# Feed-forward of a transformer layer: the full square of each relu block made by ScalarE instead of GpSimd

## The chip, the cores and the metric

One core of a Trainium2 chip runs the whole layer in one launch. The metric is the device time of that launch in microseconds; the time of the kernel before is the median of three runs, 1094.78 us. Its five engines work side by side and meet at semaphores: TensorE (PE, matmuls and weight loads), VectorE (DVE), ScalarE (ACT), GpSimd (POOL) and SyncE (SP, which issues the DMAs).

## What is computed

A pre-norm layer on x of 4 x 2048 rows of 256: attention in a window of 128 keys with one global key (16 heads of 16), then a feed-forward with ternary weights, a low-rank term and a squared relu.

```python
x = x + attention(layernorm(x), Wq, Wk, Wv, Wo)
# feed-forward on xn = layernorm(x): 256 -> 1024 -> 256
h = bitlinear(xn, w_fc) + gate * (xn @ v.T @ fast_b.T @ u.T)
r = maximum(h, 0.0)
x = x + bitlinear(r * r, w_proj)
```

## The kernel before

The program has three stages: projections (to about 124 us), attention (to about 722 us) and the feed-forward (`stage_feed`, to the end). The change is in the feed-forward alone. There the 8192 rows are cut into 16 groups of 512 (`G`), and the 1024 hidden columns into 8 blocks of 128 (`MH`, index j). Every tile of a block is 128 partitions x 512 elements.

Products run in a fast matmul format, so a value that needs full precision is split in two: a high part (rounded, fp32r) and a low part (value minus high part), with a matmul for each. For the square this takes four steps per block, and the texts below use these short names:

- **T(j)**, `pe_ternary` and `pe_low` (L1827, L1828, L1832): five matmuls that make block j of h in one of two PSUM banks, `h_bank[j % 2]`. T(j) waits until relu j-2 has read that bank (`s_r`).
- **r(j)**, L1879, ScalarE: relu from PSUM into `f_relu`. **hi(j)**, L1882, ScalarE: its Square, rounded, into `f_square_hi`; it waits for r(j).
- **sq(j)**, L1890, GpSimd: r times r in full fp32, into `f_square`; it waits for r(j).
- **lo(j)**, L1936, VectorE: `f_square` minus `f_square_hi` into `f_square_lo`; it waits for hi(j) and sq(j). **O(j)**, `pe_output` (L1846, L1848): eight matmuls with both parts; it waits for lo(j).

The tiles of r, hi, sq and lo are rings of four blocks. Each engine takes its work in the order in which it is written; nothing else orders it. One step of the loop (`body`) handles the feed-forward of group q.g, the layernorm of the group after it (`qx`) and the output projection of attention of the group after that (`qa`):

- TensorE: low-rank product (L1818, L1819), T(0), T(1), eight transposes (L1784), T(2), T(3), O(0), T(4), O(1), T(5), O(2), T(6), O(3), T(7), O(4), eight transposes (L1796), O(5), 24 matmuls of the output projection (L257 to L259), O(6), O(7).
- ScalarE: the copy of the low-rank product f_z (L1872), r and hi of blocks 0 and 1, a square root for the layernorm (L161, "the root"), r(2), hi(2), two copies f_o_t_hi (L1861), r and hi of blocks 3 to 7, two copies f_xt_hi (L1867).
- VectorE: the output rows of the group before, the low part of f_z, layernorm statistics (L146, L154, L157), lo(0), lo(1), a chain of five small operations on 4 elements (L167 to L175), lo(2), two low parts (L1902), lo(3), scaling (L247), lo(4), scaling, lo(5) to lo(7), two low parts (L1923), two sums (L1910).
- GpSimd: sq(j) and nothing else, for j = 0 to 7.

Steps 0 to 13 have both `qa` and `qx`; step 14 has no `qa` (no transposes L1784, no copies L1861), step 15 has neither.

Of the kernel before, what the change touches and what calls it, by code (L numbers as in the profile page):

```python
# [24 lines left out]
ACT = mybir.ActivationFunctionType  # L25
ALU = mybir.AluOpType
# [10 lines left out]
MH = HID // P  # L37
# [4 lines left out]
G = N // GT  # L42
# [49 lines left out]
def wait(eng, sem, value):  # L92

    if value > 0:
        eng.wait_ge(sem, value)
# [1595 lines left out]
class Feed:  # L1691
# [182 lines left out]
    def act_squares(self, act, q, j):  # L1874
        sh = self.sh
        act.wait_ge(self.s_h, q.g * MH + j + 1)
        wait(act, self.s_sq, q.g * MH + j + 1 - 4)
        wait(act, self.s_y, q.g * MH + j + 1 - 4)
        act.activation(sh.r[:, j % 4, :], self.h_bank[j % 2][:], ACT.Relu, scale=self.w.mag[:, j:j + 1]  # L1879
                       ).then_inc(self.s_r, 1)  # L1880
        act.wait_ge(self.s_r, q.g * MH + j + 1)
        act.activation(sh.r2_hi[:, j % 4, :], sh.r[:, j % 4, :], ACT.Square).then_inc(self.s_r2hi, 1)  # L1882

    def pool_squares(self, pool, q, j):
        sh = self.sh
        pool.wait_ge(self.s_r, q.g * MH + j + 1)
        wait(pool, self.s_r2lo, q.g * MH + j + 1 - 4)
        pool.tensor_tensor(sh.r2[:, j % 4, :], sh.r[:, j % 4, :], sh.r[:, j % 4, :], ALU.mult).then_inc(self.s_sq, 1)  # L1890

# [69 lines left out]
def stage_feed(block, feed):  # L1963

    sh, norm = feed.sh, feed.norm
    LX, LF, LB = 1, 2, 3

    def steps(body):
        for i in range(LF, G + LB):
            body(lambda lag, i=i: Group(i - lag) if 0 <= i - lag < G else None)

    @block.sync
    def _(sp):
        feed.load_o(sp, Group(1))
        feed.load_x(sp, Group(1))
        feed.load_o(sp, Group(2))
        feed.load_x(sp, Group(2))  # L1980

        def body(at):
            if q := at(LB):
                if q.g == G - 1:
                    feed.store_last(sp, q)
                else:
                    feed.store(sp, q)
            if q := at(-1):
                feed.load_o(sp, q)
                feed.load_x(sp, q)  # L1990
                if q.g == 4:
                    feed.store_attention(sp)

        steps(body)
        for i in range(4):

            sp.wait_ge(feed.s_out[i], DMA * (G // 4 + (i == (G - 1) % 4)))

    @block.gpsimd
    def _(pool):  # L2000
        for g in range(G):
            for j in range(MH):
                feed.pool_squares(pool, Group(g), j)

    @block.tensor
    def _(pe):
        def body(at):
            qa, qx, qf = at(0), at(LX), at(LF)
            if qf:
                feed.pe_low_rank(pe, qf)  # L2010
                feed.pe_ternary(pe, qf, 0)
                feed.pe_ternary(pe, qf, 1)
                feed.pe_low(pe, qf, 0)
                feed.pe_low(pe, qf, 1)
            if qa:
                feed.pe_turn_o(pe, qa, qf)
            if qf:
                for j in range(2, MH):
                    feed.pe_ternary(pe, qf, j)
                    feed.pe_low(pe, qf, j)  # L2020
                    if j >= 3:
                        feed.pe_output(pe, qf, j - 3)
            if qx:
                feed.pe_turn_norm(pe, qx)
            if qf:
                feed.pe_output(pe, qf, MH - 3)
            if qa:
                feed.pe_attention(pe, qa)
            if qf:
                feed.pe_output(pe, qf, MH - 2)  # L2030
            if qf and qf.g == G - 1:

                for c in range(2):
                    feed.pe_output(pe, qf, MH - 1, (c,))
            elif qf:
                feed.pe_output(pe, qf, MH - 1)

        steps(body)

    @block.scalar  # L2040
    def _(act):
        def body(at):
            qa, qx, qf = at(0), at(LX), at(LF)
            if qf:
                feed.act_z_high(act, qf)
            for j in range(MH):
                if qf:
                    feed.act_squares(act, qf, j)
                if j == 1 and qx:
                    norm.root(act, qx)  # L2050
                if j == 2 and qa:
                    feed.act_o_high(act, qa)
            if qx:
                feed.act_norm_high(act, qx)

        steps(body)

    @block.vector
    def _(dve):
        def body(at):  # L2060
            qa, qx, qf, qb = at(0), at(LX), at(LF), at(LB)
            if qb and qb.g == G - 1:
                feed.dve_last(dve, qb)
            elif qb:
                feed.dve_scaled(dve, qb)
            if qf:
                feed.dve_z_low(dve, qf)
            if qb and qb.g < G - 1:
                feed.dve_final(dve, qb)
            if qx:  # L2070
                feed.dve_front(dve, qx)
            if qf and qf.g == 0:
                sh.dve_denominators(dve, Unit(UNITS - 1))
            for j in range(MH):
                if qf:
                    feed.dve_square_low(dve, qf, j)
                if j == 1 and qx:
                    norm.rstd(dve, qx)
                if j == 2 and qa:
                    feed.dve_o_low(dve, qa)  # L2080
                if j in (3, 4) and qx:
                    feed.dve_scale(dve, qx, range((j - 3) * 2, (j - 3) * 2 + 2))
            if qx:
                feed.dve_norm_low(dve, qx)
            if qa:
                feed.dve_x1(dve, qa)

        steps(body)


def layer(nc, x, wq, wk, wv, wo, fast_b, w_fc, w_proj, u, v, gate, out):
    q_dram = nc.dram_tensor("q_parts", [G, PARTS, HD, UPG // KT, NQ, KT, GT], BF16, kind="Internal").ap()
    k_dram = nc.dram_tensor("k_parts", [G, PARTS, HD, UPG // KT, NQ, KT, KGT], BF16, kind="Internal").ap()
    va_dram = nc.dram_tensor("v_ones", [N, VROW], F32, kind="Internal").ap()
    o_dram = nc.dram_tensor("attention", [N, D], F32, kind="Internal").ap()
    with ExitStack() as outer:
        row = outer.enter_context(nc.sbuf_tensor("row", [B, H, HD], F32))
        band = outer.enter_context(nc.sbuf_tensor("band", [P, -(-WINDOW // 16) * 16], BF16))
        with ExitStack() as place:
            weights = Weights(nc, outer, wo, fast_b, w_fc, w_proj, u, v, gate)  # L2100
            sh = Shared(nc, outer, place, row, band, Weights.WORDS)
        stage_project(nc, x, (wq, wk, wv), q_dram, k_dram, va_dram, o_dram, weights, sh)
        sh.keep(nc, outer)
        feed = Feed(nc, outer, x, o_dram, sh, weights, out)
        block = outer.enter_context(nc.Block())
        stage_attend(nc, outer, block, q_dram, k_dram, va_dram, o_dram, sh, weights, feed)
        stage_feed(block, feed)
# [22 lines left out]
```

## Time and profile before

| | |
|---|---|
| three runs | 1094.78, 1091.4, 1096.73 us |
| the profiled execution | 1093.67 us, of which the span of the core is 1091.9 us |
| busy over the span | PE 96%, DVE 84%, ACT 71%, POOL 64% |
| one group of the feed-forward | 23.07 us: PE 22.76, DVE 19.42, ACT 12.98, POOL 9.09 us busy |

The engines overlap, so their busy times do not add up to the span. What counts is which engine the others wait for at a given place, and what it waits for.

### The profile page before, as it was taken

The numbers are of one execution on the slowest core, as the hardware profiler recorded it, in microseconds if no ns is written. First come the engines' busy times: TensorE is split into PE (matmuls) and PEld (weight loads), VectorE is DVE, ScalarE is ACT, GpSimd is POOL, SyncE is SP. The second block draws the span as 40 slices with busy tenths as digits, with TensorE's granted clock in tenths as the row PEclk, the third lists the DMA queues.
The fourth block names the chain that finished last, engine by engine and source line by source line (L and its number), as shares of the span: only waits on it lengthen the run. The fifth ranks groups of instructions, "written<-read, shape, count | busy, mean of one in ns | idle before, by whom it ended". The sixth has DMA issues, their size and how long they took to land.

```text
span 1091.9 us, 40107 instructions
## 1 busy us (share of the span) xinstructions
PE 1043.6 (96%) x16091; PEld 788.7 (72%) x16091; DVE 918.9 (84%) x3205; ACT 772.6 (71%) x1325; POOL 700.3 (64%) x948
## 2 busy tenths in 40 slices
PE   9999998899999999999999999779999999999997
PEld 8888885456665666556665666458888888888887
DVE  7889965799899998999989999368878888888885
ACT  7989984488788878888878888645545655456654
POOL 3665559388889888998888888734334444334443
PEclk9999998699999999999999999989999999999999
DMA  6999989656767667666767752412122311113101
GB/s 206 282 306 275 288 231 231 131 118 122 146 145 152 139 131 156 149 137 132 154 126 156 138 119 69 138 39 78 59 59 75 99 59 59 59 59 97 40 21 39
DMA packets 185290, 142.34 MB, mean 130 GB/s; under 512 B 59896, under 2 KB 184848, under 8 KB 185104
## 3 DMA queue, kind: packets, MB, share of 16 engines
q1 hardware_dynamic: 185104, 139.77, 53.0%
q8 instruction: 127, 2.08, 0.9%
q14 instruction: 59, 0.48, 0.2%
HBM read 87.98 MB, written 50.95 MB: 127 GB/s over the span
## 4 chain that ended last, share of the span: by engine, by line
PE 62%; DVE 12%; issue 4%; ACT 2%; DMA 1%; POOL 1%; SPq 0%; POOLq 0%; DVEq 0%
PE e_psum L1534 14%; PE e_psum L1556 12%; PE e_psum L1509 10%; PE e_psum L1846 6%; PE e_psum L1848 6%; DVE a_masked L1665 5%; PE e_psum L1828 3%; PE e_psum L1827 3%; DVE n_stats L146 2%; DVE f_x L1960 2%; PE e_psum L1832 1%; PE e_psum L259 1%; PE e_psum L258 1%; ACT a_weights L1622 1%; PE e_psum L1796 1%
## 5 line engine op out<-in xcount | busy, mean ns | idle before, releaser
L1622 ACT ACTIVATE a_weights<-e_psum 128x1024 f32<-128x1024 f32 (+1 forms) x512 | 391.8, 809 | 86.0 <-PE e_psum L1534 85.7
L1665 DVE CUSTOM_DVE_ANT_0 a_masked<-e_psum,band 128x290 f32<-128x290 f32 (+8 forms) x1024 | 399.8, 445 | 44.2 <-PE e_psum L1509 37.9
L1439 POOL TENSOR_SCALAR_AFFINE_SELECT a_weights<-a_weights 128x1024 f32<-128x1024 f32 x256 | 273.4, 1092 | 52.3 <-ACT a_weights L1622 51.3
L1890 POOL TENSOR_TENSOR f_square<-f_relu 128x512 f32<-128x512 f32 x128 | 146.3, 1144 | 209.4 <-ACT f_relu L1879 186.7
L1509 PE MATMUL e_psum<-e_k,e_q 96*32 96x290 bf16 (+2 forms) x4096 | 233.3, 289 | 14.9 <-DVE a_max L1665 7.3
L1534 PE MATMUL e_psum<-e_q,e_k 128*32 128x256 bf16 (+2 forms) x5632 | 239.4, 280 | 7.3 <-ACT a_weights L1622 4.3
L1556 PE MATMUL e_psum<-a_weights,a_v 128*17 128x384 f32 (+2 forms) x2816 | 219.9, 392 | 7.7 <-DVE e_turned L1291 6.4
L1534 PEld LDWEIGHTS e_psum<-e_q,e_k 128*32 128x32 bf16 x5632 | 128.1, 96 | 101.8 <-ACT a_weights L1622 44.7
L1509 PEld LDWEIGHTS e_psum<-e_k,e_q 96*32 96x32 bf16 x4096 | 113.1, 97 | 86.0 <-DVE a_max L1665 51.6
L1846 PE MATMUL e_psum<-w_w_t,f_square_hi 128*128 128x256 f32 x512 | 129.3, 287 | 5.7 <-DVE f_square_lo L1936 5.7
L1848 PE MATMUL e_psum<-w_w_t,f_square_lo 128*128 128x256 f32 x512 | 126.7, 282 | 0.0
L1879 ACT ACTIVATE f_relu<-e_psum,w_mag 128x512 f32<-128x512 f32 x128 | 87.3, 682 | 54.2 <-PE e_psum L1832 54.2
L1936 DVE TENSOR_TENSOR f_square_lo<-f_square,f_square_hi 128x512 fp32r<-128x512 f32 x128 | 98.4, 788 | 24.2 <-POOL f_square L1890 24.2
L1846 PEld LDWEIGHTS e_psum<-w_w_t,f_square_hi 128*128 128x128 f32 x512 | 96.6, 189 | 15.1 <-DVE f_square_lo L1936 12.1
L1827 PE MATMUL e_psum<-f_xt_hi,w_w_t 128*128 128x512 f32 x256 | 102.7, 401 | 1.1 <-ACT f_relu L1879 1.1
L1828 PE MATMUL e_psum<-f_xt_lo,w_w_t 128*128 128x512 f32 x256 | 101.3, 396 | 0.0
L1848 PEld LDWEIGHTS e_psum<-w_w_t,f_square_lo 128*128 128x128 f32 x512 | 96.8, 189 | 2.8
L1556 PEld LDWEIGHTS e_psum<-a_weights,a_v 128*17 128x17 f32 x2816 | 77.9, 98 | 26.7 <-issue 11.1
L1665 DVE DVE_READ_ACCUMULATOR2_ANT a_max<- 128x1 f32 x1024 | 85.6, 84 | 0.0
L1882 ACT ACTIVATE f_square_hi<-f_relu 128x512 fp32r<-128x512 f32 x128 | 80.9, 632 | 4.1
L463 POOL TENSOR_TENSOR p_q_parts<-p_rest,p_q_parts 128x512 bf16<-128x512 f32 x32 | 38.3, 1197 | 69.8 <-ACT p_q_parts L628 69.7
L1872 ACT ACTIVATE f_z<-e_psum 128x512 fp32r<-128x512 f32 x16 | 9.6, 599 | 90.6 <-PE e_psum L1819 90.6
(218 smaller groups left out, 1916.9 us busy)
## 6 DMA issues: line engine op xcount, KB each, us to landing
k_parts<-p_k_parts SPq DMA_DIRECT2D x48, 258.0 KB, 4.4
e_k<-k_parts SPq DMA_DIRECT2D x64, 193.5 KB, 3.7
q_parts<-p_q_parts SPq DMA_DIRECT2D x48, 256.0 KB, 5.2
e_q<-q_parts SPq DMA_DIRECT2D x64, 192.0 KB, 3.8
v_ones<-p_va SPq DMA_DIRECT2D x16, 544.0 KB, 5.7
e_k<-k_parts SPq DMA_DIRECT2D x64, 129.0 KB, 3.5
p_x<-in_x SPq DMA_DIRECT2D x16, 512.0 KB, 6.4
e_q<-q_parts SPq DMA_DIRECT2D x64, 128.0 KB, 3.8
```

Of the source, the lines that this page charges most:

```text
L1439: pool.affine_select(out=blocks, in_=blocks, compare_op=ALU.is_ge, fill=0.0, base=0, pattern=[[0, NQ // 2 * HEAD_COLS // P // CUT_STEP], [ ...
L1509: ins = pe.matmul(sh.tile_bank(j)[h * SUB:(h + 1) * SUB, lo:hi], qw[ux.q][0:SLOT_ROWS, h, j * SUB:(j + 1) * SUB], kt[ux.hq][0:SLOT_ROWS, h ...
L1534: ins = pe.matmul(score[third // 2][i:i + SUB, c0:c0 + m * P], kt[us.hq][:, h, k0 + i:k0 + i + SUB], qw[us.q][:, h, qb * P:(qb + m) * P], ...
L1556: ins = pe.matmul(sum_bank[32 * j:32 * j + VW, qb * P:(qb + m) * P], vw[:, (up.g * TB + kb) % V_RING, h * VW:h * VW + VW], pe_w[:, up.upar ...
L1622: act.activation(pe_w[:, us.upar, lo:hi], score[c % 2][:], ACT.Exp).then_inc(s_exp, 1)
L1665: dve.tensor_tensor_reduce(out=masked[:, place + lo:place + hi], in0=bank[:, lo:hi], in1=band[:, lo:hi], scale=1.0, scalar=NEG, op0=ALU.ad ...
L1827: pe.matmul(self.h_bank[j % 2][:], lhs, self.sh.xt_hi[:, q.par, k, :], start=(k == 0), stop=False)
L1828: pe.matmul(self.h_bank[j % 2][:], lhs, self.sh.xt_lo[:, q.par, k, :], start=False, stop=False)
L1846: pe.matmul(y, sh.r2_hi[:, j % 4, part], self.w.w2_t[:, j, :], start=(j == 0 and t == 0), stop=False, skip_group_check=True)
L1848: ins = pe.matmul(y, sh.r2_lo[:, j % 4, part], self.w.w2_t[:, j, :], start=False, stop=(j == MH - 1), skip_group_check=True)
L1890: pool.tensor_tensor(sh.r2[:, j % 4, :], sh.r[:, j % 4, :], sh.r[:, j % 4, :], ALU.mult).then_inc(self.s_sq, 1)
L1936: dve.tensor_tensor(sh.r2_lo[:, j % 4, :], sh.r2[:, j % 4, :], sh.r2_hi[:, j % 4, :].bitcast(F32), ALU.subtract).then_inc(self.s_r2lo, 1)
```

## The change

ScalarE makes sq(j) itself, as a second Square activation right behind hi(j). GpSimd's loop is gone, and it does nothing in this stage. The wait that GpSimd had, for lo(j-4) (the tile of `f_square` is free again), stands now on ScalarE in front of sq(j). The wait of r(j) for sq(j-4) is dropped, since both are on one engine.

```diff
     def act_squares(self, act, q, j):
         sh = self.sh
         act.wait_ge(self.s_h, q.g * MH + j + 1)
-        wait(act, self.s_sq, q.g * MH + j + 1 - 4)
         wait(act, self.s_y, q.g * MH + j + 1 - 4)
         act.activation(sh.r[:, j % 4, :], self.h_bank[j % 2][:], ACT.Relu, scale=self.w.mag[:, j:j + 1]
                        ).then_inc(self.s_r, 1)
         act.wait_ge(self.s_r, q.g * MH + j + 1)
         act.activation(sh.r2_hi[:, j % 4, :], sh.r[:, j % 4, :], ACT.Square).then_inc(self.s_r2hi, 1)
-
-    def pool_squares(self, pool, q, j):
-        sh = self.sh
-        pool.wait_ge(self.s_r, q.g * MH + j + 1)
-        wait(pool, self.s_r2lo, q.g * MH + j + 1 - 4)
-        pool.tensor_tensor(sh.r2[:, j % 4, :], sh.r[:, j % 4, :], sh.r[:, j % 4, :], ALU.mult).then_inc(self.s_sq, 1)
+        wait(act, self.s_r2lo, q.g * MH + j + 1 - 4)
+        act.activation(sh.r2[:, j % 4, :], sh.r[:, j % 4, :], ACT.Square).then_inc(self.s_sq, 1)
...
-    @block.gpsimd
-    def _(pool):
-        for g in range(G):
-            for j in range(MH):
-                feed.pool_squares(pool, Group(g), j)
```

On ScalarE, the start of the first feed-forward group stood so (the name in brackets is the tile or semaphore that the instruction waits for):

```order
 L1872 ACTIVATE f_z<-e_psum 128x512 [waits f_z]
-L1879 ACTIVATE f_relu<-e_psum,w_mag 128x512 [waits f_hidden]
-L1882 ACTIVATE f_square_hi<-f_relu 128x512 [waits f_relu]
-L1879 ACTIVATE f_relu<-e_psum,w_mag 128x512 [waits f_hidden]
-L1882 ACTIVATE f_square_hi<-f_relu 128x512 [waits f_relu]
+L1878 ACTIVATE f_relu<-e_psum,w_mag 128x512 [waits f_hidden]
+L1881 ACTIVATE f_square_hi<-f_relu 128x512 [waits f_relu]
+L1883 ACTIVATE f_square<-f_relu 128x512
+L1878 ACTIVATE f_relu<-e_psum,w_mag 128x512 [waits f_hidden]
+L1881 ACTIVATE f_square_hi<-f_relu 128x512 [waits f_relu]
+L1883 ACTIVATE f_square<-f_relu 128x512
```

Each pair has become a triple, and every instruction behind it on ScalarE moves back by one more activation. The root, r(2) and the copies L1861 come next; between the start of the group and r(3), which stands behind those copies, three activations have been put in: sq(0), sq(1) and sq(2).

```order
 L1861 ACTIVATE f_o_t_hi<-e_psum 128x512 [waits f_attn,f_o_turned] x2
-L1879 ACTIVATE f_relu<-e_psum,w_mag 128x512 [waits f_hidden]
-L1882 ACTIVATE f_square_hi<-f_relu 128x512 [waits f_relu]
-L1879 ACTIVATE f_relu<-e_psum,w_mag 128x512 [waits f_y,f_square,f_hidden]
-L1882 ACTIVATE f_square_hi<-f_relu 128x512 [waits f_relu]
...
+L1878 ACTIVATE f_relu<-e_psum,w_mag 128x512 [waits f_hidden]
+L1881 ACTIVATE f_square_hi<-f_relu 128x512 [waits f_relu]
+L1883 ACTIVATE f_square<-f_relu 128x512
+L1878 ACTIVATE f_relu<-e_psum,w_mag 128x512 [waits f_y,f_hidden]
+L1881 ACTIVATE f_square_hi<-f_relu 128x512 [waits f_relu]
+L1883 ACTIVATE f_square<-f_relu 128x512 [waits f_square_lo]
```

From block 4 on, the wait for f_square has left the relu, and the new Square waits for f_square_lo. On GpSimd, all 128 of its operations behind the attention are gone:

```order
 L1485 TENSOR_TENSOR e_o<-e_num,e_rden 128x16x16
-L1999 UNCONDITIONAL_BRANCH
-L1890 TENSOR_TENSOR f_square<-f_relu 128x512 x128
-L2096 UNCONDITIONAL_BRANCH
+L2083 UNCONDITIONAL_BRANCH
```

The order of instructions on TensorE, VectorE and SyncE is the same in both kernels.

## Rows read from the trace of the kernel before

**Rows 1.** The page, part 1: busy us, share of the span, instructions.

```profile
PE 1043.6 (96%) x16091; PEld 788.7 (72%) x16091; DVE 918.9 (84%) x3205; ACT 772.6 (71%) x1325; POOL 700.3 (64%) x948
```

**Rows 2.** Busy time by engine in one group (PE, PEld, DVE, ACT, POOL, clock).

```profile
794.87:817.94 23.07, 22.76 (x149) 20.32 (x149) 19.42 (x39) 12.98 (x22) 9.09 (x8) 1.00 0.24 69
```

**Rows 3.** The waits of 746 to 1080 us: total, times, longest.

```profile
ACT n_stddev L161 <- DVE n_var_eps L157: 7.2, 14, 0.5
PE e_psum L1846 <- DVE f_square_lo L1936: 4.3, 14, 0.3
```

**Rows 4.** Timeline of ScalarE in that group: start, duration, [idle before].

```profile
795.14 0.60 ACT L1872 ACTIVATE f_z<-e_psum 128x512 fp32r<-128x512 f32 x1 [6.02 <-PE e_psum L1819]
797.24 0.69 ACT L1879 ACTIVATE f_relu<-e_psum,w_mag 128x512 f32<-128x512 f32 x1 [1.51 <-PE e_psum L1832]
797.96 0.63 ACT L1882 ACTIVATE f_square_hi<-f_relu 128x512 fp32r<-128x512 f32 x1
798.50 0.67 ACT L1879 ACTIVATE f_relu<-e_psum,w_mag 128x512 f32<-128x512 f32 x1
799.20 0.63 ACT L1882 ACTIVATE f_square_hi<-f_relu 128x512 fp32r<-128x512 f32 x1
800.35 0.20 ACT L161 ACTIVATE n_stddev<-n_var_eps 128x4 f32<-128x4 f32 x1 [0.51 <-DVE n_var_eps L157]
800.46 0.67 ACT L1879 ACTIVATE f_relu<-e_psum,w_mag 128x512 f32<-128x512 f32 x1
801.16 0.63 ACT L1882 ACTIVATE f_square_hi<-f_relu 128x512 fp32r<-128x512 f32 x1
801.70 1.07 ACT L1861 ACTIVATE f_o_t_hi<-e_psum 128x512 fp32r<-128x512 f32 x2
802.65 0.69 ACT L1879 ACTIVATE f_relu<-e_psum,w_mag 128x512 f32<-128x512 f32 x1
...
818.20 0.60 ACT L1872 ACTIVATE f_z<-e_psum 128x512 fp32r<-128x512 f32 x1 [6.02 <-PE e_psum L1819]
```

**Rows 5.** Timeline of TensorE in that group: first matmuls of T(2) to T(5), O(0).

```profile
798.06 0.47 PE L1827 MATMUL e_psum<-f_xt_hi,w_w_t 128*128 128x512 f32 x1
...
799.31 0.41 PE L1827 MATMUL e_psum<-f_xt_hi,w_w_t 128*128 128x512 f32 x1
...
800.26 0.39 PE L1832 MATMUL e_psum<-f_z,w_u_t 128*128 128x512 f32 x1
800.96 0.38 PE L1846 MATMUL e_psum<-w_w_t,f_square_hi 128*128 128x256 f32 x1 [0.31 <-DVE f_square_lo L1936]
...
802.01 0.39 PE L1827 MATMUL e_psum<-f_xt_hi,w_w_t 128*128 128x512 f32 x1
...
804.13 0.39 PE L1827 MATMUL e_psum<-f_xt_hi,w_w_t 128*128 128x512 f32 x1
```

**Rows 6.** Timeline of VectorE in that group, around lo(0) and lo(1).

```profile
799.54 0.77 DVE L157 TENSOR_SCALAR n_var_eps<-n_meanvar 128x4 f32<-128x4 f32 x1
800.23 1.28 DVE L1936 TENSOR_TENSOR f_square_lo<-f_square,f_square_hi 128x512 fp32r<-128x512 f32 x2
```

**Rows 7.** Timeline of the first group (g = 0): the root's table load, r(3), T(5).

```profile
729.62 1.28 ACT L161 ACT_TABLE_LOAD   x1
...
733.22 0.69 ACT L1879 ACTIVATE f_relu<-e_psum,w_mag 128x512 f32<-128x512 f32 x1
...
734.95 0.39 PE L1827 MATMUL e_psum<-f_xt_hi,w_w_t 128*128 128x512 f32 x1
```

**Rows 8.** Timeline of the last group (g = 15): r(1), T(3).

```profile
1072.42 0.67 ACT L1879 ACTIVATE f_relu<-e_psum,w_mag 128x512 f32<-128x512 f32 x1
...
1073.17 0.47 PE L1827 MATMUL e_psum<-f_xt_hi,w_w_t 128*128 128x512 f32 x1
```

**Rows 9.** One source line's instructions: duration in ns min/median/max.

```profile
L157 DVE TENSOR_SCALAR n_var_eps<-n_meanvar x16: 169/769/772, 703.5 to 1053.3; 128x4 f32<-128x4 f32 x16
```

**Rows 10.** The page, part 5: busy, mean ns of one | idle before.

```profile
L1882 ACT ACTIVATE f_square_hi<-f_relu 128x512 fp32r<-128x512 f32 x128 | 80.9, 632 | 4.1
```

## The prediction

> **What bounds the kernel now.** The page's busy shares come first: PE is busy 96% of the span, GpSimd 64%, ScalarE 71% [rows 1]. The change lies in the feed-forward alone, so the whole-span shares decide nothing; I went to one group there. Two successive copies of f_z start at 795.14 and 818.20, so a group takes 23.06 us [rows 4]. In such a window PE is busy 22.76 us, DVE 19.42, ACT 12.98, POOL 9.09, and the granted clock is 1.00 [rows 2]. So TensorE sets the pace. It is idle 0.31 us per group, and the waits name the place: O(0) waits for lo(0), 14 times, 4.3 us in all, 0.31 each [rows 3, 5]. The reader should take from this that TensorE has no other idle time in a steady group: delay put in front of it behind O(0) has nothing to be absorbed by.
>
> ScalarE has 10 us of slack in 23, which looks like ample room for eight more Squares. But the slack is not spread evenly: 6.02 us of it lie before f_z and 1.51 before r(0), while from r(0) to r(3) ScalarE runs back to back except for the wait of the root for L157, 0.51 us [rows 3, 4]. T(2) and T(3) are released by r(0) and r(1), T(4) and T(5) by r(2) and r(3). So the question is read from that opening stretch, block by block.
>
> **What the change costs on ScalarE.** The price of sq(j) is what it adds from start to start. It is the same operation, shape and source as hi(j), only the output is f32. hi(0) starts at 797.96 and r(1) at 798.50; hi(1) at 799.20, and hi(2) at 801.16 with the copy behind it at 801.70: 0.54 us from one start to the next [rows 4], less than the 0.63 that one lasts, since neighbours overlap. I take c = 0.54 us. No row has a Square behind a Square. From below, two copies from PSUM take 0.95 us from 801.70 to 802.65, 0.475 each [rows 4]. From above, if it did not overlap, it would cost its mean of 632 ns [rows 10] and the usual gap of 0.03 us (797.24 + 0.69 to 797.96 [rows 4]), 0.66. The wait for lo(j-4) in front of it is met long before: lo(0) and lo(1) are done by 801.51 [rows 6], and sq(4) comes some 3 us behind the 803.66 worked out for r(3) below.
>
> The Trainium skill, "ScalarE: Activation LUTs", section "What ACT_TABLE_LOAD costs", prices an activation with immediate scale and bias at 186 ns + 0.833 ns per element, and lets neighbours overlap by 93 ns. For 512 elements that would be an estimate of 0.52 us, and the sum below would be about 6.1 us by it instead of 7.0; the trace's 0.54 decides.
>
> **A steady group, walked with c = 0.54** (before-times from [rows 4, 5]).
> - r(0) stays at 797.24, T(2) at 798.06.
> - r(1) comes one c later, and T(3) with it: 799.31 + 0.54 = 799.85. T(3) takes 800.26 - 799.31 + 0.23 (a matmul's pace) = 1.18, so it ends at 801.03.
> - O(0) started at 800.96, waiting for lo(0). sq(0) is done at 798.50 + 0.63 = 799.13, before DVE turns to lo(0) at 800.23 [rows 6], so lo(0) is no later. O(0) starts at 801.03 without a wait. Before, O(0) took 802.01 - 800.96 = 1.05, of which 0.10 is the refilled first matmul (0.38 against 0.28); now 0.95. T(4) starts at 801.98 against 802.01. T(3)'s delay has eaten exactly the idle time of 0.31 and the refill, so it costs nothing.
> - r(3): hi(1) 799.74, sq(1) 800.28, root 800.82 (L157 ended at 800.31, so its wait is gone), r(2) + 0.11 = 800.93, hi(2) + 0.70 = 801.63, sq(2) 802.17, copies 802.71, r(3) + 0.95 = 803.66, end + 0.69 = 804.35. T starts about 0.13 after its relu ends (797.24 + 0.69 to 798.06), so T(5) can start at 804.48. In short: three Squares add 1.62, the root's vanished hole gives back 0.61.
> - TensorE would be ready for T(5) at 801.98 + (804.13 - 802.01) = 804.10. It waits 0.38 and refills (0.47 against 0.39, 0.08): T(5) is in effect at 804.56 against 804.13, **0.43 us late**.
> - From there TensorE's pace is 2.12 us a block and ScalarE's 0.72 + 0.54 + 0.54 = 1.80, so ScalarE catches up and T(6), T(7) don't wait. At the end of the group ScalarE stood idle for 6.02 us before the next f_z [rows 4]; the five Squares behind r(3), 2.7 us at most, leave it more than 3. Nothing later in the group gives the 0.43 back.
>
> Groups 1 to 13 are alike: 13 x 0.43 = 5.6 us.
>
> **The others.** Group 0: the root's table load stands right behind hi(1) (729.62), so there is no hole to fill; r(3) moves by all of 1.62, from 733.22 to 734.84, ends 735.53, and T(5) is in effect at 735.53 + 0.13 + 0.08 = 735.74 against 734.95 [rows 7]: 0.8. Group 14 has no copies L1861 in front of r(3), 0.95 less: no wait at T(5); about 0. Group 15 has neither root nor wait at O(0): T(3) follows r(1) closely (1072.42 + 0.67, then 1073.17 [rows 8]) and moves by 0.54 and a refill, 0.6, which TensorE carries to the end.
>
> **Sum:** 5.6 + 0.8 + 0 + 0.6 = 7.0 us. Against the profiled execution's own 1093.67 us that is 1100.7; that execution lies 1.1 below the median of the runs, by which it would be 1101.8. I say 1101.3. With c = 0.475 T(5) is 3 x 0.065 earlier, 0.24 late: 3.1 + 0.6 + 0.5 = 4.2 us. With c = 0.66 it is 0.79 late: 10.3 + 1.2 + 0.7 = 12.2 us.
>
> **What VectorE gains, and why I book nothing.** With GpSimd idle some DVE operations should shorten: L157 on 4 elements lasts 769 ns in the median and 169 at best [rows 9] in this stage, so something holds it 0.6 us. The Trainium skill, "GPSIMD Engine Reference", section "Key points", says that GpSimd shares its SBUF interfaces with VectorE and contends with instructions in a 2-port mode or with two SBUF inputs; by it DVE gets shorter, and the trace agrees as far as L157 goes. lo(0) may end at 800.3 instead of 800.9. But by then TensorE is in T(3) until 801.03.
>
> **Rivals.**
> 1. *Faster: the freed VectorE decides* (0.05). If T(3) and T(5) were not late, O(0) would start at 800.49 instead of 800.96 and without refill, 0.57 a group, 7.4 over 13: about 1086. Both hang on c. O(0)'s gain is 0.57 - c; T(5), 3c - 1.19 late, passes zero at c = 0.39 us. Below that the kernel is faster. No activation on 512 elements in these rows costs under 0.475.
> 2. *No change: the delay is absorbed* (0.14). c near 0.4, or the root slipping in where I don't see it: 1093 to 1097. For it speaks ScalarE's average slack of 10 us; against it that TensorE has only 0.31 us idle in a group, already spent.
> 3. *Dearer: the Squares don't overlap* (0.09). If each Square waited out the one before as hi(j) waits for r(j) (0.72), T(5) would be 0.97 late: 12.6 + 1.3 + 0.8 = 14.7, about 1109. Only from c = 0.86 (2.12 - 0.72 - 0.54) on would ScalarE be the bound throughout a group, and nothing points there.
>
> **How the numbers follow.** The forecast, with c between 0.475 and 0.66, has 0.72. A difference under 0.5% (5.5 us) can't be told from none here; c under about 0.50 falls within it, some 0.16 of the 0.72. So slower 0.56 + 0.09 = 0.65, same 0.14 + 0.16 = 0.30, faster 0.05. The range, 1096 to 1106.5, leaves out rival 1, rival 3 and part of rival 2, and takes in 4.2 to 12.2 us on the run's own time.
>
> **What would show it.** In the profile after: start to start of 0.54 us from hi(j) to the new Square and on to the next; a group of 23.5 us instead of 23.07; no wait of O(0) for lo(0) but one of T(5) for r(3), about 0.4 us, in 14 groups; L157 at about 0.17 us; the root waiting for nothing. The prediction is wrong if the group stays at 23.1 us, if T(5) isn't where TensorE waits, or if c is off.

## The result, and the profile after

The changed kernel took 1097.39 us (median of 20 runs) against 1091.71 us of the kernel before (20 runs). The ratio is 1.0051, 95% interval 1.0034 to 1.0068, some 5.6 us slower (3.7 to 7.4 by the interval). The profiled execution's span is 1096.1 us.

The page after, part 1, answers to [rows 1]:

```profile
PE 1046.5 (95%) x16091; PEld 789.9 (72%) x16091; DVE 871.6 (80%) x3205; ACT 829.7 (76%) x1453; POOL 554.1 (51%) x820
```

The window of one steady group after (time from one f_z to the next, then PE, PEld, DVE, ACT, POOL, clock) answers to [rows 2]:

```profile
795.36:818.74 23.38, 23.02 (x149) 20.47 (x148) 16.41 (x38) 16.57 (x31) 0.00 (x0) 1.00 0.22 69
```

ScalarE is busier by 3.6 us a group, GpSimd by 9.1 less, and VectorE by 3.0 less although it has the same work. The group is longer by 0.31 us, all the same at a granted clock of 1.00. Where that comes from is read on the timelines. ScalarE after, the same stretch as [rows 4] (start, duration, [idle before]):

```profile
795.36 0.60 ACT L1872 ACTIVATE f_z<-e_psum 128x512 fp32r<-128x512 f32 x1 [5.04 <-PE e_psum L1819]
797.46 0.69 ACT L1878 ACTIVATE f_relu<-e_psum,w_mag 128x512 f32<-128x512 f32 x1 [1.51 <-PE e_psum L1832]
798.18 0.63 ACT L1881 ACTIVATE f_square_hi<-f_relu 128x512 fp32r<-128x512 f32 x1
798.72 0.61 ACT L1883 ACTIVATE f_square<-f_relu 128x512 f32<-128x512 f32 x1
799.24 0.67 ACT L1878 ACTIVATE f_relu<-e_psum,w_mag 128x512 f32<-128x512 f32 x1
...
801.00 0.19 ACT L161 ACTIVATE n_stddev<-n_var_eps 128x4 f32<-128x4 f32 x1
801.09 0.67 ACT L1878 ACTIVATE f_relu<-e_psum,w_mag 128x512 f32<-128x512 f32 x1
...
802.85 1.06 ACT L1861 ACTIVATE f_o_t_hi<-e_psum 128x512 fp32r<-128x512 f32 x2
803.80 0.69 ACT L1878 ACTIVATE f_relu<-e_psum,w_mag 128x512 f32<-128x512 f32 x1
```

TensorE after (first matmuls of T(3), O(0), T(4) and T(5)), beside [rows 5]:

```profile
799.96 0.50 PE L1827 MATMUL e_psum<-f_xt_hi,w_w_t 128*128 128x512 f32 x1 [0.26 <-ACT f_relu L1878]
...
801.23 0.28 PE L1846 MATMUL e_psum<-w_w_t,f_square_hi 128*128 128x256 f32 x1
...
802.18 0.39 PE L1827 MATMUL e_psum<-f_xt_hi,w_w_t 128*128 128x512 f32 x1
...
804.54 0.50 PE L1827 MATMUL e_psum<-f_xt_hi,w_w_t 128*128 128x512 f32 x1
804.88 0.40 PE L1828 MATMUL e_psum<-f_xt_lo,w_w_t 128*128 128x512 f32 x1
```

Read both from the start of f_z, so that the two kernels can be laid over each other. r(3) comes 8.44 us after f_z; before it came at 7.51. O(0) starts after 5.87 us without a wait; before it was 5.82 with a wait of 0.31. T(4) starts at 6.82 against 6.87: the delay of T(3) has cost nothing by then. T(5) starts at 9.18 against 8.99, and after its wait its second matmul comes 0.34 us behind the first instead of 0.23 (the texts call this 0.11 us the refill). That makes 0.30 of the group's 0.31.

The waits of 746 to 1080 us after name the same place (who waited for whom: total, times, longest). The wait of O(0) for lo(0) of [rows 3] and that of the root for L157 are gone; in their stead T waits longer for a relu. Before, 17 of its weight loads waited, those of T(3) in 15 groups (0.2 us each) and of T(2) in the two last ones:

```profile
PEld e_psum L1827 <- ACT f_relu L1879: 4.8, 17, 1.0
```

After, there are 30: T(3) again, but 0.70 us in each steady group, T(2) again, and T(5) in 13 groups, 0.30 us each:

```profile
DVE f_square_lo L1929 <- ACT f_square L1883: 67.6, 99, 1.4
PEld e_psum L1827 <- ACT f_relu L1878: 16.5, 30, 1.0
PE e_psum L1827 <- ACT f_relu L1878: 5.2, 17, 0.5
```

And L157, held in the kernel before [rows 9], runs at its shortest everywhere:

```profile
L157 DVE TENSOR_SCALAR n_var_eps<-n_meanvar x16: 170/170/171, 703.4 to 1056.9; 128x4 f32<-128x4 f32 x16
```

**The books of the stage.** From the first f_z to the end it took 367.0 us before and 372.3 after. Of these 5.3 us, 4.1 lie in groups 1 to 13 (13 x 0.31), 0.67 in group 0 (24.77 against 24.10), -0.06 in group 14 (20.13 against 20.19) and 0.59 behind the last f_z (23.43 against 22.84). In that last group there are no copies in front of r(3) and T(5) doesn't wait; there T(3) is the one that is late. The stages ahead of it hold the same work in both; the profiled executions differ there by 1.1 us the other way (first f_z at 724.9 before, 723.8 after), which is why the spans differ by 4.2 only.

### The profile page after: what moved, and what is told of

Same layout as the page of the kernel before. It is cut to its first block, busy times and chain, and to the rows that moved or that the text cites. A ratio compares the mean times of both kernels' runs of the same rounds, so it can differ in the third digit from the quotient of the medians.

```text
span 1096.1 us, 39983 instructions
## 1 busy us (share of the span) xinstructions
PE 1046.5 (95%) x16091; PEld 789.9 (72%) x16091; DVE 871.6 (80%) x3205; ACT 829.7 (76%) x1453; POOL 554.1 (51%) x820
## 4 chain that ended last, share of the span: by engine, by line
PE 60%; ACT 9%; DVE 7%; issue 4%; DMA 2%; SPq 1%; POOL 1%; ACTq 0%; POOLq 0%; DVEq 0%
PE e_psum L1534 13%; PE e_psum L1556 12%; PE e_psum L1509 9%; DVE a_masked L1665 5%; PE e_psum L1846 5%; PE e_psum L1848 5%; PE e_psum L1827 4%; PE e_psum L1828 4%; ACT f_relu L1878 3%; ACT f_square L1883 2%; PE e_psum L1832 2%; ACT a_weights L1622 1%; PE e_psum L259 1%; PE e_psum L258 1%; PE e_psum L257 1%
## 5 line engine op out<-in xcount | busy, mean ns | idle before, releaser
L1929 DVE TENSOR_TENSOR f_square_lo<-f_square,f_square_hi 128x512 fp32r<-128x512 f32 x128 | 88.7, 693 | 80.2 <-ACT f_square L1883 80.2
L1827 PE MATMUL e_psum<-f_xt_hi,w_w_t 128*128 128x512 f32 x256 | 105.7, 413 | 7.9 <-ACT f_relu L1878 6.7
L1883 ACT ACTIVATE f_square<-f_relu 128x512 f32<-128x512 f32 x128 | 78.8, 615 | 0.0
```

Source lines behind the costliest of these rows:

```text
L1827: pe.matmul(self.h_bank[j % 2][:], lhs, self.sh.xt_hi[:, q.par, k, :], start=(k == 0), stop=False)
L1883: act.activation(sh.r2[:, j % 4, :], sh.r[:, j % 4, :], ACT.Square).then_inc(self.s_sq, 1)
```

## The experiments

The measure in all of them is the length of a steady group, from one f_z to the next on ScalarE. In the kernels before and after it repeats to 0.02 us from group to group, while whole runs of one kernel differ by several us. Ratios are to the kernel before.

| kernel | group, us | first f_z to end, us | ratio (95%) |
|---|---|---|---|
| before | 23.07 | 367.0 | |
| changed | 23.38 | 372.3 | 1.0051 (1.0034 to 1.0068) |
| e1, full Square behind the next relu | 22.72 | 362.7 | 0.9963 (0.9945 to 0.9982) |
| e2, copies on VectorE | 23.02 | 366.9 | 1.0000 (0.9976 to 1.0024) |
| e3, blocks 0 to 2 on GpSimd | 23.07 | 367.1 | 1.0002 (0.9977 to 1.0027) |
| e4, blocks 3 to 7 on GpSimd | 23.38 | 372.2 | 1.0048 (1.0024 to 1.0072) |
| e5, GpSimd busy beside | 23.38 | 372.5 | 1.0036 (1.0015 to 1.0057) |
| e6, half Squares | 22.79 | 363.4 | 0.9962 (0.9937 to 0.9987) |
| e7, Squares twice | 26.27 | 423.2 | one run, 1150.58 us |
| e8, e1 with GpSimd busy beside | 23.35 | 372.4 | one run, 1098.37 us |
| e9, e1 for blocks 0 to 4 only | 22.72 | 362.3 | 0.9948 (0.9922 to 0.9973) |

**Which of the eight Squares cost: e3 and e4.** Both split the blocks between the engines. The table at the top of e3 says which of the eight blocks ScalarE squares; in e4 it is the other way round, and each engine counts on a semaphore of its own.

```diff
+SQ_ON_ACT, SQ_COUNT, SQ_EACH = (0, 0, 0, 1, 1, 1, 1, 1), (1, 2, 3, 1, 2, 3, 4, 5), (3, 5)
...
+        if SQ_ON_ACT[j]:
+            wait(act, self.s_r2lo, q.g * MH + j + 1 - 4)
+            act.activation(sh.r2[:, j % 4, :], sh.r[:, j % 4, :], ACT.Square).then_inc(self.s_sqs[1], 1)
```

> Full squares of blocks 0, 1, 2 by GpSimd as before the change, of blocks 3 to 7 by ScalarE as after. Theory: the five behind r(3) are free, since ScalarE is faster per block than TensorE; a group takes 23.07 us, as before. Rival (cost goes by the number of Squares on ScalarE): five eighths of the 0.31 us, a group of 23.26.

> The reverse: full squares of blocks 0, 1, 2 by ScalarE, of blocks 3 to 7 by GpSimd. Theory: the whole loss is here; a group takes 23.38 us as after, with the wait at T(5). Rival (by number): three eighths of 0.31, 23.19 us.

23.07 and 23.38 us: the five Squares behind r(3) cost nothing, the three in front of it cost all. Counting Squares would have given 23.26 and 23.19. In e3 the old wait is back, in e4 it is that of the changed kernel. From the waits of e3, and behind it of e4:

```profile
PEld e_psum L1848 <- DVE f_square_lo L1944: 10.3, 14, 0.7
```

```profile
PEld e_psum L1829 <- ACT f_relu L1881: 15.7, 29, 1.0
```

**Which of the two delayed relus costs: e2.** The Squares stay on ScalarE, and its two copies in front of r(3) go to VectorE.

```diff
# scalar
-                if j == 2 and qa:
-                    feed.act_o_high(act, qa)
# vector
                 if j == 2 and qa:
+                    wait(dve, feed.s_a, (qa.g - 1) * 2 + 2)
+                    feed.dve_o_high(dve, qa)
                     feed.dve_o_low(dve, qa)
```

> The changed kernel with the two copies f_o_t_hi made by VectorE in front of the low parts instead of ScalarE, which takes 0.95 us from in front of r(3) and puts about 1.3 us on VectorE, which waits a lot by now. Theory: the wait at T(5) and its refill go, the delay of T(3) stays as hidden as it is: a group of about 23.03 us, kernel about 1.001 of before. Rival (the delay of T(3) is what costs): a group stays at 23.38.

23.02 us. With r(3) early, the wait at T(5) goes: the weight loads that wait for a relu fall from 30 to 17, those of T(3) and the two T(2):

```profile
PEld e_psum L1827 <- ACT f_relu L1878: 12.6, 17, 1.0
PE e_psum L1827 <- ACT f_relu L1878: 5.2, 17, 0.5
```

T(3) is as late as in the changed kernel and costs nothing in a steady group. So the loss of a steady group hangs on r(3) alone. Behind the last f_z, where T(3) is late and the copies don't stand, e2 takes 23.36 us, near the changed kernel's 23.43 and not the 22.84 of before.

**How it depends on a Square's price: e6 and e7.** In e6 each full Square covers the first 256 columns (the other half of the tile stays at zero); in e7 it is made twice.

```diff
# e6
-        act.activation(sh.r2[:, j % 4, :], sh.r[:, j % 4, :], ACT.Square).then_inc(self.s_sq, 1)
+        act.activation(sh.r2[:, j % 4, :GT // 2], sh.r[:, j % 4, :GT // 2], ACT.Square).then_inc(self.s_sq, 1)
# e7
+        act.activation(sh.r2[:, j % 4, :], sh.r[:, j % 4, :], ACT.Square).then_inc(self.s_twice, 1)
+        act.wait_ge(self.s_twice, q.g * MH + j + 1)
         act.activation(sh.r2[:, j % 4, :], sh.r[:, j % 4, :], ACT.Square).then_inc(self.s_sq, 1)
```

> The changed kernel with each full Square on the first 256 of its 512 columns; the other half of the full square is left at zero, so that the output is wrong. The added cost c of a Square falls from 0.52 to about 0.26 to 0.30 us. Theory: c is under the 0.39 us at which T(5) stops waiting, and T(3) is late by less than the idle time in front of O(0): a group of about 22.8 us, shorter than before the change. Rival (any work added on ScalarE in the group costs in proportion): half of 0.31, 23.2 us.

> The changed kernel with each full Square made twice, the second after the first has ended: c is about 1.2 us. Theory: r(3) comes another 3 x 0.7 = 2.1 us later, and with 0.72 + 0.54 + 1.2 = 2.46 us a block ScalarE is slower than TensorE's 2.12, so T(6) and T(7) wait too, 0.34 each: a group of about 26.2 us. Rival (ScalarE's slack of 5 us in a group absorbs more): under 25 us.

The half Square costs 0.31 us from start to start; ScalarE in e6:

```profile
795.00 0.40 ACT L1884 ACTIVATE f_square<-f_relu 128x256 f32<-128x256 f32 x1
795.31 0.67 ACT L1879 ACTIVATE f_relu<-e_psum,w_mag 128x512 f32<-128x512 f32 x1
```

At 0.31 us a group takes 22.79, less than before the change; at 0.52 it takes 23.38; with the double Square (0.65 from the first to the second, then 0.54) 26.27. A price in proportion, 0.15 for half of 0.31, is excluded: the sign turns between 0.31 and 0.52, and the prediction's 0.39 lies between them (its own 1.19 / 3 is 0.40; worked back from the measured 0.31 us of loss it would be 0.52 - 0.31 / 3 = 0.42, an estimate). At 1.19 us ScalarE's 0.70 + 0.54 + 1.19 = 2.43 a block is more than TensorE's 2.12, and ScalarE sets the pace of the blocks.

**What the idle GpSimd gives: e5.** The changed kernel, with GpSimd multiplying a tile that nobody reads.

```diff
+    @block.gpsimd
+    def _(pool):
+        pool.memset(feed.own[:], 1.0).then_inc(feed.s_own, 1)
+        pool.wait_ge(feed.s_own, 1)
+        for g in range(G):
+            for j in range(MH):
+                pool.wait_ge(feed.s_r, g * MH + j + 1)
+                pool.wait_ge(feed.s_own, g * MH + j + 1)
+                pool.tensor_tensor(feed.own[:], feed.own[:], feed.own[:], ALU.mult
+                                   ).then_inc(feed.s_own, 1)
```

> The changed kernel, and GpSimd multiplies a tile of its own by itself (128x512 f32, 128 times, each released by the relu of its block), on which nobody waits. It brings back what GpSimd does to VectorE and nothing else. Theory: VectorE's operations lengthen again (L157 to 0.77 us), lo(0) ends about 0.6 us later, just about when T(3) ends, and the group stays at 23.38 to 23.45 us. Rival (the idle GpSimd gives something back, so that the Squares' true price is more than 0.31 us): a group of 23.6 us or more.

The group stays at 23.38, as the theory said; but L157 stayed at 0.17 us, which it did not say. The timelines of VectorE and of GpSimd in e5 show why:

```profile
799.40 0.17 DVE L157 TENSOR_SCALAR n_var_eps<-n_meanvar 128x4 f32<-128x4 f32 x1
...
801.75 0.80 DVE L169 TENSOR_TENSOR n_newton<-n_var_eps,n_rstd_first 128x4 f32<-128x4 f32 x1
```

```profile
799.63 1.45 POOL L2002 TENSOR_TENSOR f_own<-f_own 128x512 f32<-128x512 f32 x1 [0.72 <-ACT f_relu L1880]
801.48 1.05 POOL L2002 TENSOR_TENSOR f_own<-f_own 128x512 f32<-128x512 f32 x1 [0.40 <-ACT f_relu L1880]
```

L157 falls between two products of GpSimd, since r(1), which releases the product of block 1, is later in this kernel. L169, which falls into a product, lasts 0.80 us on 4 elements and ends at 802.55, just when GpSimd's ends (802.53). The kernel before shows the same:

```profile
799.25 1.04 POOL L1890 TENSOR_TENSOR f_square<-f_relu 128x512 f32<-128x512 f32 x1 [0.20 <-ACT f_relu L1879]
801.21 1.20 POOL L1890 TENSOR_TENSOR f_square<-f_relu 128x512 f32<-128x512 f32 x1 [0.92 <-ACT f_relu L1879]
801.43 0.17 DVE L167 RECIPROCAL n_rstd_first<-n_stddev 128x4 f32<-128x4 f32 x1
801.63 0.80 DVE L169 TENSOR_TENSOR n_newton<-n_var_eps,n_rstd_first 128x4 f32<-128x4 f32 x1
```

L157 ended at 799.54 + 0.77 = 800.31 [rows 6], GpSimd's product of block 1 at 800.29; L169 ended at 802.43, the product of block 2 at 802.41. So L157 and L169 are held until GpSimd's operation is over. Not every small operation is: L167, of the same size and inside the same product, took its usual 0.17 us in all groups. No run here shows why.

In e5 VectorE is busy 261 us of 746 to 1080, in the changed kernel 232, before 280. So e5 brings back 29 of the 48 us, and the group is as long as without them: in this order of work this relief of VectorE is worth nothing.

**Putting the Squares where ScalarE waits: e1.** Between r(j) and hi(j) ScalarE waits for its own relu to end (0.70 to 0.72 us from start to start, against the 0.52 to 0.54 after a Square). e1 puts the full Square of the block before into that gap, and so behind the relu for which TensorE waits.

```diff
         act.activation(sh.r[:, j % 4, :], self.h_bank[j % 2][:], ACT.Relu, scale=self.w.mag[:, j:j + 1]
                        ).then_inc(self.s_r, 1)
+        if j > 0:
+            self.act_full_square(act, q, j - 1)
         act.wait_ge(self.s_r, q.g * MH + j + 1)
         act.activation(sh.r2_hi[:, j % 4, :], sh.r[:, j % 4, :], ACT.Square).then_inc(self.s_r2hi, 1)
+        if j == MH - 1:
+            self.act_full_square(act, q, j)
```

> ScalarE's order changed: the full Square of block j-1 is issued between relu j and the rounded Square j, where ScalarE otherwise waits for its own relu. Theory (what a Square costs is decided by the relu that stands behind it, r(1) for T(3) and r(3) for T(5)): r(1) is not delayed, so T(3) is not; GpSimd is still idle, so lo(0) ends at about 5.3 us after the start of f_z and O(0) follows T(3) without a wait; only sq(0) and sq(1) stand before r(3), which comes at about 7.5 us after f_z instead of 8.44. A group takes about 22.5 us (after: 23.38, before: 23.07), the kernel about 0.992 of before. Rival (ScalarE's eight added Squares cost by their sum, wherever they stand): a group stays at about 23.4.

22.72 us a group, 0.9963 of the kernel before: the direction is the theory's, the size is not (22.5 and 0.992 were expected). ScalarE and TensorE in e1:

```profile
790.77 0.60 ACT L1872 ACTIVATE f_z<-e_psum 128x512 fp32r<-128x512 f32 x1 [5.28 <-PE e_psum L1819]
...
794.70 0.62 ACT L1890 ACTIVATE f_square<-f_relu 128x512 f32<-128x512 f32 x1
795.22 0.62 ACT L1883 ACTIVATE f_square_hi<-f_relu 128x512 fp32r<-128x512 f32 x1
...
798.40 0.70 ACT L1878 ACTIVATE f_relu<-e_psum,w_mag 128x512 f32<-128x512 f32 x1
```

```profile
796.17 0.39 PE L1846 MATMUL e_psum<-w_w_t,f_square_hi 128*128 128x256 f32 x1
```

r(3) comes 7.63 us after f_z, near its old 7.51. But sq(0) ends at 795.32, lo(0) at 796.11, and O(0) starts at 796.17, 5.40 us after f_z, not 5.3, and with a refill (0.39 instead of 0.28). Against the expected 22.5 that is about 0.05 for the later start and 0.11 for the refill; O(2) loses another 0.07 or 0.08 in the same way (its second matmul comes 0.20 us behind the first instead of 0.12). Together they are the missing 0.22.

**Where e1's gain comes from: e8.** e1 and the GpSimd loop of e5 together.

> The reordered kernel (full Square behind the next relu) with GpSimd multiplying a tile of its own, 128 times, each released by the relu of its block. The question is where the reordered kernel's gain over the kernel before comes from. Theory: from VectorE, which GpSimd no longer holds up in front of lo(0): with GpSimd busy again at the times of before, L157 is held until the operation of block 1 ends, O(0) waits for lo(0) again, and a group goes back from 22.72 to about 23.1 us. Rival (the gain comes from the Squares' ending earlier than GpSimd's products did): a group stays at 22.72 us.

The gain is gone and more: 23.35 us. L157 is held again, O(0) waits for lo(0) again, and lo(2) is held as well (1.04 us), which went beyond the 23.1 expected. TensorE (O(0)), VectorE and GpSimd in e8:

```profile
801.31 0.39 PE L1848 MATMUL e_psum<-w_w_t,f_square_hi 128*128 128x256 f32 x1 [0.30 <-DVE f_square_lo L1938]
```


```profile
799.89 0.77 DVE L157 TENSOR_SCALAR n_var_eps<-n_meanvar 128x4 f32<-128x4 f32 x1
800.58 0.68 DVE L1938 TENSOR_TENSOR f_square_lo<-f_square,f_square_hi 128x512 fp32r<-128x512 f32 x1
...
804.70 1.04 DVE L1938 TENSOR_TENSOR f_square_lo<-f_square,f_square_hi 128x512 fp32r<-128x512 f32 x1 [0.67 <-ACT f_square L1892]
```

```profile
799.60 1.04 POOL L2009 TENSOR_TENSOR f_own<-f_own 128x512 f32<-128x512 f32 x1 [0.20 <-ACT f_relu L1880]
```

So in e1's order a busy GpSimd costs 0.63 us a group, and in that of the changed kernel nothing. O(0) starts 5.82 us after f_z again, as in the kernel before, which takes back e1's whole gain of 0.35; the other 0.28 is at O(2), which waits for the held lo(2), a wait that the kernel before does not have. So the rival is out, and the 0.63 is no measure of what the change of the engine gained. An idle GpSimd pays only when TensorE is really waiting for VectorE.

**The end: e9.** In e1 the last group's tail was 0.6 us longer than before (23.44 against 22.84); sq(6) stands there in front of hi(7). e9 moves the Squares of blocks 0 to 4 only.

```diff
+        if 0 < j < 6:
+            self.act_full_square(act, q, j - 1)
...
+        if j >= 5:
+            self.act_full_square(act, q, j)
```

> The reordered kernel, but the full Squares of blocks 5, 6 and 7 stand directly behind their own rounded Square, since ScalarE has caught up with TensorE there and waits anyway. Theory: the steady group stays at 22.72 us; in the last group, where nothing covers the end, lo(7) comes about 0.4 us earlier and the stretch from the last f_z to the end falls from 23.44 to about 23.0 us. Ratio to before about 0.996, as the reordered kernel. Rival (r(7) is late in every group): a group of over 22.8 us.

The steady group stays at 22.72, the tail falls to 23.04 us, so that 0.4 of the 0.6 lay in that order; where the other 0.2 lies is open. The ratio is 0.9948 (0.9922 to 0.9973). e1's 0.9963 lies in that interval, so that the 0.4 us between them show in the profiles only. e9 is faster than the kernel before, by about half a percent, and than the changed one.

## Why the prediction was right

- **The bound and the place.** TensorE sets the pace, and only the opening of a group matters: shown by e3 and e4, which put all of a steady group's loss in the three Squares in front of r(3), and by e2, which puts it at r(3). T(5) waits in the 14 groups that were forecast: in groups 1 to 13, and in group 0 (0.56 us).
- **T(3) late, at no cost.** O(0) starts without a wait and T(4) at 6.82 us after f_z against 6.87 before (6.84 was worked out). That the numbers meet so closely is in part luck, two misses of opposite sign: T(3) starts at 4.60 and not at 4.71, since it had 0.09 us to spare before (its weight load could start at 799.22, its matmul started at 799.31) and the Square is cheaper by 0.02; and it takes 1.27 us and not 1.18, since after its wait it refills as well, which the prediction left out. e2, which leaves T(3) late, is at 23.02.
- **T(5) late.** Right in its place, too large in its size: 0.43 us forecast, 0.31 measured (0.30 at the second matmul). Of the difference 0.08 is ScalarE's: the new Square costs 0.52 us from its start to the next (798.72 to 799.24), not hi's 0.54, three times, and the root 0.09 instead of 0.11. Another 0.08 is the way from a relu's end to T: 803.80 + 0.69 = 804.49 to 804.54 is 0.05, where the prediction took 0.13 from T(2), which has transposes in front of it as well. Against that the refill is 0.11, not 0.08. The wait itself is 0.24 us beyond the point at which TensorE would have been ready (6.82 + 2.12 = 8.94), where 0.38 was forecast.
- **The Trainium skill's figure** ("ScalarE: Activation LUTs", section "What ACT_TABLE_LOAD costs") gave an estimate of 0.52 us for the Square; this case's trace agrees, 0.52. It was closer than the row of hi(j).
- **The other groups.** Group 0 0.67 against 0.8 forecast, group 14 -0.06 against 0, group 15 0.59 against 0.6.
- **The sum.** 5.3 us in the profile and 5.6 by the ratio, against 7.0. The prediction drew its line between slower and the same at 5.5 us; the interval, 3.7 to 7.4, is clear of zero but lies on both sides of that line, so the direction is shown and that class is not. The forecast of 1101.3 lies 3.9 above the median of 1097.39, of which 1.4 to 1.7 is this excess; the rest is that it started from runs at 1093.67 and 1094.78, while the kernel before has its median over 20 runs at 1091.71. Both errors point upwards, and the measured time lies 1.4 us above the lower end of the stated range.
- **VectorE's gain booked at nothing.** Right for this kernel, and shown by e5 (23.38 with and without). The condition of rival 1, a Square under 0.39 us, is borne out in its sign by e6, where 0.31 us gives 22.79. "GPSIMD Engine Reference" of the Trainium skill, section "Key points", says that the two engines share interfaces; what the traces here add is the form that it takes on small operations: L157 and L169 are held until GpSimd's has ended, while L167 is not held at all.
- **Rivals 2 and 3.** The delay of r(3) was not absorbed (that of T(3) was, as forecast), and the Squares do overlap (0.61 us long, 0.52 from start to start). e7 shows that 1.19 us a Square is past the point at which ScalarE bounds the group.

## What to carry to other kernels

An engine's average slack says little about what more work on it costs: ask which of its instructions another engine waits for, and count only what is put in front of those. Here eight Squares with 10 us of room cost 0.31 us a group, by three of them in front of one relu, and the same Squares moved behind the relus made the kernel about 0.4% faster than it had been. Taking an engine out of contention pays only if what it was slowing is what the bound engine waits for, so the change and the order of the work have to be fitted together.

## What the runs showed of the hardware

Two VectorE operations on 128x4, L157 and L169, last 0.76 to 0.82 us instead of 0.16 or 0.17 when they start inside a GpSimd product of 128x512, and end within 0.04 us of its end; the reciprocal L167 keeps its 0.17 us inside the same product. In e5 and e8 GpSimd's tile is used by nobody else, so that it isn't a matter of shared data. GpSimd's product is longer too when it starts while VectorE is in lo(0): 1.45 us in e5 against 1.04.

A relu that the next activation waits for is followed by it after 0.70 to 0.72 us, a Square that the next waits for after 0.64 or 0.65 (e7); an activation that doesn't wait for the one before follows after 0.48 to 0.57. The gap takes most of another activation: in e1 relu, Square and rounded Square take 1.61 or 1.62 us a block (798.40 to 800.02 by the starts of two relus), where the changed kernel takes 1.76 to 1.78.
